# A graph-network kernel: key gathers of 64 bytes a partition in place of 32, and every row of dst lanes loaded as bytes

## The reference

```
# block 0, for every edge (s, d):
h(a, b) = relu([a, b] @ W1.T + b1) @ W2.T + b2          # 32 -> 64 -> 16
F_s = I - 2 v v^T / |v|^2 with v = h(x_s, x_d);  F_d likewise with h(x_d, x_s)
L = -F_s^T F_d;   coef = deg^-1/2[s] * deg^-1/2[d]
out = x - scatter_add(src, coef * L x_d) - scatter_add(dst, coef * L^T x_s)
x = layernorm(x + relu(out))
# block 1, twice with tanh:
h = tanh(segment_sum over dst of (h @ W)[src] * norm, plus self loops, + b)
x = layernorm(x + h)
```

## Time and profile before

| what | value |
|---|---|
| median of three runs | 7017.48 us (7016.65 to 7027.73) |
| span of the profiled execution | 7361.5 us |
| DVE busy over the span | 6335.9 us, 86% |
| ACT busy | 4842.1 us, 66% |
| PE busy | 4369.6 us, 59% |
| POOL busy | 2840.7 us, 39% |
| first expansion, 1403 to 2348 us | 945 us |

### The profile page before, as it was taken

How to read it: one execution, slowest core, us unless ns; L and a number is a source line. 1 busy time by engine, 2 the same in 40 slices (tenths; PEclk the granted TensorE clock), 3 DMA queues, 4 the chain that set the end, 5 groups by cost and what they waited for, 6 DMA issues and landing times.

```text
span 7361.5 us, 242681 instructions
## 1 busy us (share of the span) xinstructions
PE 4369.6 (59%) x83922; PEld 3504.3 (48%) x83922; DVE 6335.9 (86%) x9628; ACT 4842.1 (66%) x13310; POOL 2840.7 (39%) x2217
## 2 busy tenths in 40 slices
PE   1442000376665888888888888766566655566554
PEld 0342000266664555555555555555456544565443
DVE  4679997344445899999999999999999999999999
ACT  1665104122222899999999999899666677566776
POOL 5222304566764222222222222278500388200686
PEclk6666555688887898999889998887765699666898
DMA  4100000488876333333333333244499644799444
GB/s 63 8 8 8 4 0 26 148 297 298 299 288 218 120 117 118 116 118 116 116 116 116 117 117 117 88 121 120 105 294 291 211 120 120 200 293 295 127 121 95
DMA packets 510685, 1043.90 MB, mean 142 GB/s; under 512 B 125636, under 2 KB 316452, under 8 KB 497540
## 3 DMA queue, kind: packets, MB, share of 16 engines
q1 hardware_dynamic: 376804, 761.05, 30.1%
q0 software_dynamic: 113920, 281.72, 15.9%
q10 hardware_dynamic: 19872, 0.11, 0.2%
HBM read 756.44 MB, written 286.18 MB: 142 GB/s over the span
## 4 chain that ended last, share of the span: by engine, by line
DVE 28%; issue 27%; PE 12%; ACT 10%; POOL 10%; DVEq 5%; ACTq 3%; another core or an unknown queue 2%; DMA 1%; SPq 0%; POOLq 0%
PE ps L1118 7%; POOL got L638 4%; POOL sw_inb L638 4%; DVE xs_ring L1864 4%; PE ps L1259 3%; DVE wide_hotb L1987 3%; DVE keys L1476 3%; DVEq L1758 3%; ACT apartb L959 2%; DVE lane_hot L1754 2%; ACT step_lo L738 2%; DVE prods L1832 2%; ACTq L1006 2%; DVE keys L1475 2%
## 5 line engine op out<-in xcount | busy, mean ns | idle before, releaser
L638 POOL DMA_INDIRECT xs_ring<-xd_rows,src_idx x488 | 595.3, 1220 | 1803.8 <-DVE xs_ring L1864 1663.8
L1987 DVE TENSOR_SCALAR wide_hotb<-sw_inb,slot_id 128x2048 bf16<-128x2048 bf16 x976 | 923.2, 1014 | 57.5 <-PE ps L1259 57.3
L1754 DVE TENSOR_TENSOR wide_hotb<-dst_key,iota_b 128x1792 bf16<-128x1792 bf16 x879 | 949.0, 1080 | 8.5 <-ACT val_out L1017 4.4
L1259 PE MATMUL ps<-wide_tabb,wide_hotb 128*128 128x48 bf16 x15616 | 640.1, 207 | 360.9 <-DVE wide_hotb L1987 232.3
L638 POOL DMA_INDIRECT got<-val_rows,dst_idx x296 | 396.7, 1340 | 1177.3 <-DMA val_rows<-val_out 1085.9
L1118 PE MATMUL ps<-row_tab,dst_hot 128*128 128x64 bf16 x15744 | 656.0, 203 | 295.7 <-issue 244.9
L1259 PEld LDWEIGHTS ps<-wide_tabb,wide_hotb 128*128 128x128 bf16 x15616 | 592.0, 112 | 409.2 <-ACT val_out L1017 315.2
L1148 PEld LDWEIGHTS ps<-wide_tab,wide_hot 128*128 128x128 bf16 x23424 | 617.8, 99 | 347.8 <-DVE wide_hot L1748 309.1
L1118 PEld LDWEIGHTS ps<-row_tab,dst_hot 128*128 128x128 bf16 x15744 | 577.1, 104 | 374.9 <-issue 340.0
L638 POOL DMA_INDIRECT src_key<-chunk_keys,src_idx x488 | 622.0, 1275 | 335.5 <-ACT xd_out L801 187.3
L1148 PE MATMUL ps<-wide_tab,wide_hot 128*128 128x32 bf16 x23424 | 642.4, 181 | 89.0 <-DVE wide_hot L1748 84.0
(11 more groups left out here) (416 smaller groups left out, 11818.9 us busy)
## 6 DMA issues: line engine op xcount, KB each, us to landing
dw_in<-dst_wide SPq DMA_DIRECT2D x96, 1312.0 KB
xd_rows<-xd_out SPq DMA_DIRECT2D x128, 984.0 KB
sw_in<-src_wide SPq DMA_DIRECT2D x244, 512.0 KB
sw_inb<-src_wide SPq DMA_DIRECT2D x244, 512.0 KB, 5.1
val_rows<-val_out SPq DMA_DIRECT2D x488, 192.0 KB, 4.1
sw_inb<-src_byte SPq DMA_DIRECT2D x244, 256.0 KB, 4.4
msg_rows<-msg_out SPq DMA_DIRECT2D x244, 200.0 KB, 2.8
dw_in<-dst_byte SPq DMA_DIRECT2D x32, 656.0 KB
```

Source lines behind the costliest of these rows:

```text
L638: return pool.indirect_dma_start(out=into, out_offset=None, in_=table, in_offset=bass.IndirectOffsetOnAxis(index, 0))
L1259: last = mm(ps_val[s * 2 + h][:, t, :], wide_hot2[s][:, half, e:e + P], wide_tab2[s][:, h, half * 3 * D:(half + 1) * 3 * D], start=half == ...
L1754: return v.tensor_tensor(to.rearrange("p t (j k) -> p t j k", k=2), rel.unsqueeze(2).to_broadcast(shape), iota_b[:, 0:w].rearrange("p (j k ...
L1987: last = v.tensor_scalar(wide_hot2[q % 2][:, half, :], sw_in2[q][:, :], slot_id[:, half:half + 1], None, ALU.is_equal)
```

## The change

Two things. The key gathers take two rows of `chunk_keys` (KEY_GOT = 16 values, 64 bytes) in place of one, starting at the row that the index names. `src_key` becomes [128, 488, 16], of which the first 8 of each 16 are read; `chunk_keys` gets one row more at its end, which is filled by a store of its own, and POOL waits for that store with the two others ahead of its marks. And `load_wide` takes all rows from `dst_byte`, so all four `dw_in` tiles are bytes. The memset of the unused end of `src_key` is dropped. `dst_wide` is still stored.

```diff
+    KEY_GOT = 2 * CH
...
-        chunk_keys = dram("chunk_keys", [P * CPR, CH])
+        chunk_keys = dram("chunk_keys", [P * CPR + KEY_GOT // CH - 1, CH])
...
-        dw_in = [sb(f"dw_in{k}", [P, WID], U8 if k == 3 else BF16, of=pc) for k in range(4)]
+        dw_in = [sb(f"dw_in{k}", [P, WID], U8, of=pc) for k in range(4)]
...
-        src_key = sb("src_key", [P, LW * CH], of=pc)
+        src_key = sb("src_key", [P, NST, KEY_GOT], of=pc)
...
+            sp.dma_start(chunk_keys[P * CPR:, :], list_keep[0:1, 0, 0:CH]).then_inc(lists_cleared, 16)
...
-            sp.dma_start(chunk_keys.rearrange("(p c) k -> p (c k)", p=P), sorted_keys[:, :]).then_inc(sorted_stored, 16)
+            sp.dma_start(chunk_keys[0:P * CPR, :].rearrange("(p c) k -> p (c k)", p=P), sorted_keys[:, :]).then_inc(sorted_stored, 16)
...
-                rows = dst_byte_v if k == 3 else dst_wide_v
+                rows = dst_byte_v
...
-            pool.wait_ge(lists_cleared, 32)
+            pool.wait_ge(lists_cleared, 48)
...
-                gather(src_key[:, s * CH:(s + 1) * CH], chunk_keys, src_idx[:, s:s + 1]).then_inc(keys_got, 16)
+                gather(src_key[:, s, :], chunk_keys, src_idx[:, s:s + 1]).then_inc(keys_got, 16)
...
-            v.memset(src_key[:, NST * CH:], 0.0)
...
-            step(v.tensor_copy(key_i[:, :], src_key[:, 0:n]))
+            step(v.tensor_copy(key_i[:, :].rearrange("p (s c) -> p s c", c=CH), src_key[:, :, 0:CH]))
```

## The result

The changed kernel is slower: 7144.71 us (7142.39 to 7148.14, 4 runs) against 7021.22 (7016.65 to 7027.73, 4 runs), ratio 1.018 with a 95% interval of 1.0168 to 1.0192, or 123.5 us more. The forecast was 7120.

The account below looks back on a forecast made before the run. In the first expansion no single engine filled the profiled 945 us; without the profiler it was taken as 825 us, bounded by POOL or DMA. After, POOL ends it at 927 us: 7017.5 + 102 = 7120 us, range 6985 to 7165.

Parts of the forecast that it names:

- POOL ends the stage: First expansion after the change: rows done by about 710 us, POOL's key gathers last, at 927 us.
- H - 0.5: Gather time POOL loses per DVE one-hot of length H: 1.08 us for bf16, 2.44 us for bytes.
- The stage of before: First expansion of the unchanged kernel without the profiler: taken as 825 us, ends 781 and 858.
- The crawl belongs to the profiled execution: First expansion: PE's issue waits on weight loads, 340 us, taken wholly or mostly as absent without the profiler.
- rival (b): POOL's gather cycle is shorter without the profiler, the 0.30 us gaps being recording: 6945 to 7046 us; chance 0.20.
- DMA holds before at 854 us: First expansion before the change: 760 us of DMA time at the later expansion's share of 0.89 gives 854 us.
- POOL at 781: First expansion before the change: POOL's 770 us plus 11 us until its first gather, as a limit of 781 us.
- forecast of 102: First expansion without the profiler: 927 us after less 825 us before, +102 us, with ends +69 and +146.
- The small edits: Extra 32-byte store, dropped src_key memset and strided key_i read: taken as 0 (store at most 2.3 us, key_i 0 to +2).
- rival (d): The wider key gather costs POOL 0.40 us more each, 197 us on top: 7317 us; chance 0.06.
- Rival (a): PE's crawl is real, so the first expansion before takes 945 us unprofiled too: -17 us, 7000 us; chance 0.17.
- Rival (c): Byte one-hots hold gathers no longer than bf16 ones, 0.88 us per row: -94 us, 6923 us; chance 0.07.

Follow-up runs that it names:

- e5: The kernel before with the second half of its key gathers left out (244 of 488): 6917.42 us, 0.9856 to before.
- e6: The kernel before with all four dw_in as bf16 and all loads from dst_wide, so no bytes: 6975.15 us, 0.9942 to before.
- e3: The kernel before with only the key gathers widened to 64 bytes, three of four rows still bf16: 7033.09 us, 1.0016 to before.
- e2: The kernel before with only the byte loads for all rows, key gathers still at 32 bytes: 7140.6 us, 1.0179 to before.
- second profile of before: The kernel before, unchanged, profiled once more: 7028.07 us (1 run), first expansion 816.0 us.
- e8: The changed kernel with each one-hot computed by two instructions of half the length, back to back: 7097.88 us, 1.0114 to before.
- e7: The kernel before with the one-hots of bf16 rows as a tensor_tensor compare in place of tensor_scalar: 7112.7 us, 1.0138 to before.

## Why the prediction was right, and where it was not

The mechanism was the one forecast, and its size too: POOL ends the stage, 927 us were forecast and 934 measured; the sum of the gathers was to be 768 us and is 756. The mean loss of 2.44 us came out as 2.31, the 1.08 of bf16 as 1.00. The rows were done at 594 us, under the 607 that the sum of DVE's times had as least (for the 710 it had as most it gives no working): a row took 4.60 us, since in the trace a one-hot and the chooses around it overlap by some 0.1 us each.

The rule behind H - 0.5 was wrong in two points, and that they cancel is luck. It had every gather that meets a one-hot end 0.12 us after it, whenever it began. The runs show that a gather begun inside the one-hot mostly ends 0.81 us after it, which costs 0.69 us more, and that one begun over 0.47 us ahead loses nothing. Neither could be seen in the two pairs of the earlier trace rows, which were both of gathers begun 0.14 to 0.33 us ahead.

The stage of before, 825 us (781 to 858), measured 816. It was right for reasons that were partly wrong: the middle between a limit that was too low and one that did not hold fell near the measured value, which is luck too.

- *The crawl belongs to the profiled execution*: right for that execution, but not by the profiler. All later profiles have spans 2 us under the time of their run. With that rival (b) falls as well: the profiled execution of after has the 0.30 us after each gather and took no longer than the other executions, so they are in the timed runs too.
- *DMA holds before at 854 us, at a share of 0.89*: wrong, mis-sized by the share. The stage sustains 0.97 (e5, e6), so the rows of before need 718 us and not 854, and DMA never was the end. Another stretch's share was no bound.
- *POOL at 781*: too low, because 770 us were taken from a trace in which POOL had often been idle when a one-hot came. The sum worked out beside it, 789 us and 13 ahead, is 802; measured are 814. With 2 us for the last keys to land, as in the 927, that sum would have put the stage's difference at 927 - 804 = 123; in the stage 934 - 816 = 118 us were measured, in the time 123.5. So the forecast of 102 was short by the 825 in the main.
- *The small edits*: nothing, as costed, for the extra store and the strided read of `key_i` (2.13 us in e3 as in before). The wide gather costs no time on POOL, as costed (e2 and after, e3 and before have the same sums within 1.4 us), and with that rival (d) falls. e3 was 11 us slower outside the stage all the same, which was not foreseen.

Rival (a), a real crawl, fell with the second profile of before. Rival (c), gathers not held, fell with after itself.

The Trainium skill, "SBUF — State Buffer", Who interferes with whom, has it that whoever issues first keeps the shared ports for the whole instruction; the gather of 1498.64 in e8 had begun 0.40 us before the DVE instruction and still was held. The trace agrees only if the gather counts as first from some 0.47 us after its start on: those further on were not held, and made the one-hot longer. The same section takes tensor_tensor with two SBUF inputs to disturb GpSimd's reads, and marks as inferred that this leaves the making of descriptors alone. In e7 it held every gather that began inside it and none that had begun 0.18 to 0.47 us ahead, which fits, if a gather reads first and writes its descriptors after; that order no run shows. The limit that the Trainium skill, "DMA: Bandwidth & Descriptors", Specifications, gives for a core from HBM, about 358 GB/s, is passed by 8% in e5: 386 GB/s over 719 us, of which the loads are one row spread over 128 partitions. So the estimate of 778 us by that page was 60 us over the 718 that the rows of before take.

## What to carry to other kernels

An indirect DMA on POOL costs its 0.94 us only when DVE lets it: sum up POOL's gathers with what each long DVE instruction that works from SBUF to SBUF adds (here its length less 0.6 to 0.7 us for tensor_scalar, less 0.8 for tensor_tensor), before you lengthen such an instruction to save DMA bytes. When POOL ends a stage, try the DVE instructions beside it in pieces of half a microsecond. Here eight pieces took 239 us off the changed kernel, and pieces with a second byte row in four took the kernel before down by 1.7% (pieces alone 1.2%). But count on it only after a run, since four pieces gave nothing on the changed kernel. And before an execution's idle time is explained, compare its span with the timed runs: 344 us too much meant that the trace was of a disturbed execution.

## What the runs showed of the hardware that was not expected

- A tensor_tensor of two SBUF tensors (2.87 us) holds an indirect DMA on POOL that begins inside it (92 of 92), but not one that began 0.18 to 0.47 us ahead (0 of 31), where a tensor_scalar of 2.94 us or of 1.57 us does hold it; a copy_predicated out of PSUM holds neither.
- A gather beside a tensor_scalar is held when it began inside it or up to 0.47 us ahead. When it began 0.47 to about 0.65 us ahead, it ends on time and the tensor_scalar takes up to 0.25 us more.
- With four byte pieces of 0.85 us a gather waited through the whole train in 86 of 128 rows (3.97 us for one gather); with eight pieces of some 0.5 us most that were held got in by the end of the third (1.12 us).
- The DMA engines moved 385 and 386 GB/s over 780 and 719 us at a share of 0.97, with broadcast loads of 10496 bytes (in the second of these stretches one of four has 5248) and stores of 7872 bytes a partition.
